# Gathering every unit's cached values by indirect transfer, copying only the keys, and moving the transposes to transfers two units earlier

## The chip, the core and the metric

The kernel runs on one core of a Trainium2 chip. Its metric is the device time of one execution in microseconds. Five engines work side by side, each on its own list of instructions: TensorE (PE in the profile; PEld is its weight load), VectorE (DVE), ScalarE (ACT), GpSimd (POOL) and SyncE (SP), which here only starts transfers. Semaphores order them. Transfers run on 16 DMA engines. They are started by SP and ACT, and, where the addresses come from an index list, by POOL.

## The reference

Two layers with residuals. For each of 8 sequences of 128 tokens with 512 features:

```python
x = x + einsum('bsi,boi->bso', x, weight[adapter_ids])      # one 512x512 matrix per sequence
q = rope(rmsnorm(x Wq^T)); k = rope(rmsnorm(x Wk^T)); v = x Wv^T   # 32 query heads, 8 key heads, D = 128
kc = k_cache[block_table].reshape(b, 512, 8, 128)           # 16 pages of 32 keys per sequence
vc = v_cache[block_table].reshape(b, 512, 8, 128)
scores = q . [kc, k] / sqrt(D), cached keys past cache_seqlens masked; probs = softmax(scores)
x = x + (probs . [vc, v]) Wo^T
```

All is float32, and the kernel keeps that accuracy by splitting each operand into a rounded high part and a low remainder and multiplying three times (high by high, high by low, low by high).

## The kernel before

The attention is cut into 64 units. Unit u is key head u // 8 with its 4 query heads, of sequence u % 8, and has 640 keys: 512 cached and 128 new. A period of the program works on several units at once. In period i TensorE makes the scores of unit i (`scores`), projects the queries and keys of unit i+1 (`project_q`, `project_kv`, then `turn_q` and `turn_k`, which transpose them), multiplies the probabilities of unit i-1 with the values (`times_v`), and projects the output of unit i-2 (`project_o`). The order of every engine's instructions is written out by hand; there is no scheduler.

The probabilities have to be transposed before they meet the values. Up to unit NA-1 (NA is 8) TensorE does it: `turn_p` makes 20 transposes of 128x128 for a unit, and ACT and DVE split what comes out. From unit NA on, ACT and DVE first split the probabilities into two 16-bit planes (`upper_plane` L817, `lower_plane` L1080), SP starts four transposing transfers (`turn_upper` L458, `turn_lower` L470), and ACT (L753) and POOL (`p_lo`, L591) read the turned planes. `LAST` (unit 63) is turned on TensorE again.

The cached keys and values come in one of two ways. Units 0 to 8 (below NL = 9) take them from the pages: SP starts 16 transfers of 16 KB for the keys (`load_kt`), and POOL four indirect gathers of 128 rows of 512 B for the values (`gather_v`, L562), partition p of tile t being key 128t + p. For all later units the kernel first makes a copy in DRAM in the order of the sequences (`copy_page` L338, 16 pages for each sequence, keys and values of the remaining heads in one transfer of 224 KB). ACT then loads a unit's keys (`load_k` L348) and SP its values (`load_v` L443), 256 KB each. The tables COPY_SP and COPY_ACT say how many groups of four pages each engine starts in each period.

GpSimd's work in a period from NA+1 on, in the order of its program, is: a part of a weight chunk if the tables put one at place 0 (`split_w(i, 0)`, which writes wl), the low part of the keys (`keys_lo`, kl), the sum of the two rotary products (`q_sum`, m), the high part of the values (`values_hi`, vh), the scales (`scales`, var and rst), the low part of the values (`values_lo`, vl), three of the five `p_lo` (ptl), a weight chunk at place 1, and the last two `p_lo`. LO_POOL gives the chunks 0 to 9 of key head h the periods 8h-5, 8h-4, 8h-3 (place 1), 8h-2 (places 0 and 1), 8h-1 (place 0), 8h (place 1), 8h+1 (places 0 and 1), and 8h+2 (place 0); LO_DVE moves a few early ones to VectorE, chunks 4 and 5 of head 1 (period 6) among them.

Of the kernel before, what the change touches and what calls it, by code (L numbers as in the profile page):

```python
# [15 lines left out]
P = 128  # L16
NB = 8
# [6 lines left out]
PSZ = 32  # L24
KEYS = 640
# [26 lines left out]
NL = NB + 1  # L52
NA = 8
# [5 lines left out]
COPY_SP = (0, 1, 1, 1, 1, 1, 1, 2, 0, 1, 1, 1, 1, 1)  # L59
COPY_ACT = (2, 2, 3, 2, 2, 3, 3, 2, 1, 0, 0, 0, 0, 0)  # L60
# [39 lines left out]
def build(nc, x, xt, lw, wall, kv, ids_lens, table, pages, qkw, consts, iota, out):  # L100
    with ExitStack() as ctx:
# [9 lines left out]
        def slots(name, n):  # L111
# [57 lines left out]

        inv_s = cst[:, 3:67]  # L170
# [59 lines left out]
        d_k, d_v, d_mask, d_lenc, d_rows = (slots("d_k", 2), slots("d_v", 2), slots("d_mask", 2),  # L230
                                            sem("d_lenc"), sem("d_rows"))
# [5 lines left out]
        c_ilf, c_tabf, c_kidx, c_kidx1, c_pos, c_ang, c_sin, c_cos = (  # L237
            sem("c_ilf"), sem("c_tabf"), sem("c_kidx"), sem("c_kidx1"), sem("c_pos"), sem("c_ang"), sem("c_sin"),
# [29 lines left out]
        copy = nc.dram_tensor("cache_rows", (2 * NK, NB, NPG, PSZ * D), F32, kind="Internal").ap()  # L268
# [52 lines left out]
        def load_kt(e, regs, v, t):  # L321
# [6 lines left out]
            for j in range(4):  # L328
# [3 lines left out]
                    kv[2 * hk + 1, bass.ds(numbers[j], 1), :].rearrange("a (p n) -> (a p) n", p=P)  # L332
                ).then_inc(d_rawk[v % 2], 16)

        def copy_page(e, b, k, number):

            rows = slice(2 if b >= NL - NB else 4, 2 * NK)
            e.dma_start(copy[rows, b, k, :].rearrange("r (s n) -> s r n", s=16),  # L338
                        kv[rows, bass.ds(number, 1), :].rearrange("r a (s n) -> (a s) r n", s=16)
                        ).then_inc(d_copy[b], 16)  # L340

        def load_k(e, v):
            hk, b = divmod(v, NB)
            if v < NL + NB:
# [4 lines left out]
                        copy[2 * hk + 1, b].rearrange("k (d r) -> d k r", r=PSZ)  # L349
# [47 lines left out]
        def _(e):  # L397
# [1303 lines left out]
```

## Time and profile before

| what | value |
|---|---|
| runs | 1002.82, 1002.83, 1006.3 us; median 1002.83 us |
| profiled execution, span from first to last instruction | 1006.6 us |
| TensorE busy | 994.3 us (99%) |
| VectorE busy | 861.5 us (86%) |
| ScalarE busy | 810.3 us (80%) |
| GpSimd busy | 795.8 us (79%) |
| bytes moved by transfers | 180.94 MB |

The profiled execution is one run of its own; no time around its span is given. Busy shares are means over the whole span. The start, the eight or so units in which TensorE transposes, and the long even part after them have different limits, so the trace is read by stretches below. A period of the even part is told in the trace by L1527, the transposing of a unit's new keys, which TensorE does once in each period.

### The profile page before, as it was taken

To read this page: it belongs to the slowest core of one execution; us is meant where nothing else is said; L and a number is where in the kernel's file an instruction comes from. 1 tells how busy PE (TensorE), PEld (TensorE's weight loads), DVE (VectorE), ACT (ScalarE), POOL (GpSimd) and SP (SyncE) were. 2 spreads that over 40 slices of the span, in tenths; PEclk is the share of its full clock that TensorE was granted. 3 is DMA by queue.
4 is the path that set the end of the run, shared out by engine and by line. 5 is a ranking of instruction groups with operands and counts; after the bars stand their busy time and mean duration, and the time that the engine had idled before them with its cause. 6 is when DMAs were issued, how large, how long until landed. Compare 5 with 4: busy or idle time off the path is not lost.

```text
span 1006.6 us, 19441 instructions
## 1 busy us (share of the span) xinstructions
PE 994.3 (99%) x5471; PEld 864.3 (86%) x5471; DVE 861.5 (86%) x1787; ACT 810.3 (80%) x2109; POOL 795.8 (79%) x811
## 2 busy tenths in 40 slices
PE   8999999999999999999999999999999999999998
PEld 6778888888888888888888888888888888888886
DVE  7676657799999899999998999899999999998995
ACT  4455456698889889888988898898888988988884
POOL 4876677497889879897898888898798978888672
PEclk9999999999999999999999999999999999999999
DMA  8999879899988888888988888888988879888873
GB/s 254 277 262 260 283 229 258 213 211 201 221 162 162 161 158 153 166 157 152 171 153 162 156 160 165 148 168 155 170 148 165 157 151 166 162 162 144 153 149 84
DMA packets 513643, 180.94 MB, mean 180 GB/s; under 512 B 429873, under 2 KB 495682, under 8 KB 513538
## 3 DMA queue, kind: packets, MB, share of 16 engines
q1 hardware_dynamic: 381280, 143.20, 68.9%
q10 hardware_dynamic: 131106, 34.15, 15.3%
q0 software_dynamic: 1152, 2.36, 0.8%
q8 instruction: 45, 0.74, 0.3%
q14 instruction: 60, 0.49, 0.2%
HBM read 105.45 MB, written 31.86 MB: 136 GB/s over the span
## 4 chain that ended last, share of the span: by engine, by line
PE 95%; DVE 2%; ACTq 1%; issue 1%; ACT 1%; another core or an unknown queue 0%; POOL 0%; DVEq 0%
PE S L1408 22%; PE O L1341 7%; PE O L1343 7%; PE O L1342 7%; PE Q L1341 6%; PE Q L1343 6%; PE Y L1341 6%; PE Q L1342 6%; PE Y L1343 6%; PE Y L1342 6%; PE T L1347 4%; PE KV L1342 3%; PE KV L1341 3%; PE KV L1343 3%; PE KV L1361 1%; PE Y L1361 1%
## 5 line engine op out<-in xcount | busy, mean ns | idle before, releaser
L1080 DVE SCALAR_TENSOR_TENSOR pr<-pr,rc,raw 128x640 f16<-128x640 f32 x220 | 258.8, 1177 | 15.3 <-ACT raw L817 8.3
L1052 DVE CUSTOM_DVE_ANT_0 pr<-S,mask,rst 128x640 f32<-128x640 f32 x256 | 225.4, 881 | 16.6 <-PE S L1408 13.3
L837 ACT ACTIVATE pr<-pr,nb 128x640 f32<-128x640 f32 x256 | 211.7, 827 | 14.5 <-DVE nb L1052 14.5
L817 ACT ACTIVATE raw<-pr,rc 128x640 f16<-128x640 f32 x220 | 176.2, 826 | 0.6 <-DVE rc L1068 0.4
L617 POOL TENSOR_TENSOR m<-m 128x512 f32<-128x512 f32 x63 | 112.5, 1786 | 73.7 <-DVE m L1119 69.8
L591 POOL TENSOR_SCALAR ptl<-first 128x512 fp32r<-128x512 f16 x140 | 111.8, 799 | 17.6 <-issue 6.0
L570 POOL TENSOR_TENSOR kl<-raw,kh 128x512 fp32r<-128x512 f32 x64 | 97.8, 1528 | 34.5 <-ACT kh L720 33.5
L1408 PE MATMUL S<-kh,qh 128*128 128x320 f32 x512 | 120.8, 317 | 3.7 <-DVE nb L1052 3.6
L591 POOL TENSOR_SCALAR ptl<-turned 128x512 fp32r<-128x512 f16 x135 | 108.3, 802 | 11.2
L1408 PE MATMUL S<-kh,ql 128*128 128x320 f32 x512 | 116.8, 309 | 0.0
L783 ACT ACTIVATE Q<-Q 128x128 f32<-128x128 f32 x256 | 68.2, 266 | 59.9 <-DVE m L1119 59.9
L1408 PE MATMUL S<-kl,qh 128*128 128x320 f32 x512 | 116.2, 308 | 0.0
L1408 PEld LDWEIGHTS S<-kh,qh 128*128 128x128 f32 x512 | 91.7, 189 | 23.8 <-issue 4.7
L1341 PE MATMUL O<-pth,vh 128*128 128x512 f32 x252 | 105.5, 419 | 0.8 <-DVE ptl L983 0.5
L1341 PE MATMUL Y<-wh,oh 128*128 128x512 f32 x252 | 104.7, 415 | 0.4 <-DVE ol L983 0.4
L1341 PE MATMUL Q<-wh,xh 128*128 128x512 f32 x256 | 101.5, 396 | 0.5 <-issue 0.5
L1343 PE MATMUL Q<-wh,xl 128*128 128x512 f32 x256 | 100.9, 394 | 0.0
L1342 PE MATMUL Q<-wl,xh 128*128 128x512 f32 x256 | 100.2, 391 | 0.0
L1342 PE MATMUL Y<-wl,oh 128*128 128x512 f32 x252 | 99.7, 395 | 0.0
L1343 PE MATMUL Y<-wh,ol 128*128 128x512 f32 x252 | 99.6, 395 | 0.0
L1343 PE MATMUL O<-pth,vl 128*128 128x512 f32 x252 | 99.2, 394 | 0.0
L1342 PE MATMUL O<-ptl,vh 128*128 128x512 f32 x252 | 98.6, 391 | 0.0
(179 smaller groups left out, 2674.9 us busy)
## 6 DMA issues: line engine op xcount, KB each, us to landing
wraw<-in_wall SPq DMA_DIRECT2D x74, 256.0 KB, 4.4
cache_rows<-in_kv ACTq DMA_DIRECT2D x80, 224.0 KB
raw<-cache_rows SPq DMA_DIRECT2D x57, 256.0 KB, 4.0
raw<-cache_rows ACTq DMA_DIRECT2D x53, 256.0 KB, 5.0
mask<-mask_rows SPq DMA_DIRECT2D x64, 128.0 KB
cache_rows<-in_kv SPq DMA_DIRECT2D x36, 224.0 KB
first<-in_lw SPq DMA_DIRECT2D x5, 1024.0 KB
cache_rows<-in_kv SPq DMA_DIRECT2D x16, 192.0 KB, 4.2
```

Source lines behind the costliest of these rows:

```text
L570: return e.tensor_tensor(dst, src, hi.bitcast(F32), ALU.subtract)
L591: e.tensor_scalar(ptl[:, i % 3, :].rearrange("p (g n) -> p g n", g=G), plane_tile(u, 1, t), 1.0 / PS, 1.0, ALU.mult, ALU.mult).then_inc(g_ ...
L617: e.tensor_tensor(m1[:, :, :], m1[:, :, :], m2[:, :, :], ALU.add).then_inc(q_added, 1)
L783: made = e.activation(part, part, ACT.Square, accum_out=ssq[:, j % 2, r:r + 1])
L817: e.activation(upper16[:, g, :], pr[:, slot(u, g), :], ACT.Copy, scale=rc[:, u % 2, g:g + 1]).then_inc(a_f1, 1)
L837: e.activation(pr[:, slot(u, g), :], pr[:, slot(u, g), :], ACT.Exp, bias=nb[:, u % 2, g:g + 1], scale=-1.0, accum_out=sm[:, u % 2, g:g + 1 ...
L1052: e.tensor_tensor_reduce(pr[:, slot(u, g), :].rearrange("p (a n) -> p a n", a=2), S[:, :, 0:320], mask[:, u % 2, :].rearrange("p (a n) -> ...
L1080: e.scalar_tensor_tensor(out=lower16(u, g), in0=pr[:, slot(u, g), :], scalar=rc[:, u % 2, g:g + 1], in1=upper16[:, g, :], op0=ALU.mult, op ...
L1341: e.matmul(dst, lh, rh, start=first, stop=False)
L1342: e.matmul(dst, lh, rl, start=False, stop=False)
L1343: return e.matmul(dst, ll, rh, start=False, stop=last)
L1408: made = e.matmul(S[:, a, 0:320], l[:, u % 2, qs], r[:, u % 2, 320 * a:320 * a + 320], start=first, stop=last)
```

## The change

- NA goes from 8 to 6, so units 6 and 7 are transposed by transfers, and NL is NA + 1 = 7, so keys come straight from the pages for units 0 to 6 only.
- `load_v` and its semaphores are gone. POOL gathers the values of all 64 units, with one indirect transfer per unit: 128 rows of 2 KB, four neighbouring keys of a page to a partition. From period 7 on it stands as the last instruction of POOL's period. In the first loop one gather takes the place of four.
- Keys in a tile are thus every fourth key of a page. The page layout of the keys in DRAM, the iota for the mask, ACT's rounding of the keys (`keys_hi`) and POOL's `keys_lo` follow this order: both now read the raw keys in runs of 8 elements.
- The copy in DRAM holds keys alone: 7 rows of 16 KB a page (8 for sequence 7) instead of 14 (12 for part of them), so 112 KB a transfer. COPY_SP and COPY_ACT spread it over 12 periods instead of 14.
- The index list has one column per unit, made on VectorE in eight small steps (`value_rows`) over the first periods, and the table of pages comes in one transfer instead of four.

```diff
-NL = NB + 1
-NA = 8
+NA = 6
+NL = NA + 1
-COPY_SP = (0, 1, 1, 1, 1, 1, 1, 2, 0, 1, 1, 1, 1, 1)
-COPY_ACT = (2, 2, 3, 2, 2, 3, 3, 2, 1, 0, 0, 0, 0, 0)
+COPY_SP = (0, 1, 1, 1, 1, 1, 1, 2, 2, 2, 2, 1)
+COPY_ACT = (2, 3, 3, 3, 3, 3, 0, 0, 0, 0, 0, 0)
...
+        def by_tile(keys):
+
+            return keys.rearrange("d (g t j) -> d t g j", g=NPG, t=NT)
+        def tiles_of(keys):
+            return keys.rearrange("d (t g j) -> d t g j", g=NPG, t=NT)
...
-            rows = slice(2 if b >= NL - NB else 4, 2 * NK)
+            rows = slice((NL - b + NB - 1) // NB, NK)
...
-            def load_v(v):
-                hk, b = divmod(v, NB)
-                if v < NL + NB:
-                    e.wait_ge(d_copy[b], 16 * NPG)
-                e.wait_ge(g_vlo, v - 1 if v <= NA else v)
-                e.dma_start(rawv[raw_at(v)], copy[2 * hk, b].rearrange(
-                    "k (r d) -> (k r) d", d=D).rearrange("(t p) d -> p t d", p=P)
-                            ).then_inc(d_v[v % 2], 16)
...
-                if NL <= i < NU:
-                    load_v(i)
...
-            def gather_v(v, t):
...
+            def gather_v(v):
+                e.wait_ge(c_kidx, v // NB + 1)
+                if v >= 2:
+                    e.wait_ge(g_vlo, v - 1 if v <= NA else v)
                 e.indirect_dma_start(
-                    out=rawv[raw_at(v)][:, t, :], out_offset=None,
...
+                    out=rawv[raw_at(v)].rearrange("p t d -> p (t d)"), out_offset=None, in_=vc,
+                    in_offset=bass.IndirectOffsetOnAxis(ap=kidx[:, v:v + 1], axis=0)
                 ).then_inc(d_rawv[v % 2], 16)
...
-                minus(kl[:, j % 2, 0:512], rawk[raw_at(j)], kh[:, j % 2, 0:512]).then_inc(g_kc, 1)
+                minus(tiles_of(kl[:, j % 2, 0:512]), by_tile(rawk[raw_at(j)]),
+                      tiles_of(kh[:, j % 2, 0:512])).then_inc(g_kc, 1)
...
                 if w < LAST:
                     p_lo(w, 3)
                     p_lo(w, 4)
+                if i < NU:
+                    gather_v(i)
...
-                rounded(kh[:, j % 2, 0:512], rawk[raw_at(j)]).then_inc(a_kc, 1)
+                rounded(tiles_of(kh[:, j % 2, 0:512]), by_tile(rawk[raw_at(j)])).then_inc(a_kc, 1)
...
-            for g in range(4):
-                e.dma_start(tabb[32 * g:32 * g + 32, :],
-                            table[g:g + 1, :].broadcast_to([32, NB * NT])).then_inc(d_tab, 16)
+            e.dma_start(tabb[:, :], table).then_inc(d_tab, 16)
```

GpSimd's list in a period of the even part with a weight chunk on both sides of the end of the period. Before:

```order
L570 TENSOR_TENSOR vl<-raw,vh 128x512
L591 TENSOR_SCALAR ptl<-turned 128x512 x3
L570 TENSOR_TENSOR wl<-wraw,wh 128x512
L591 TENSOR_SCALAR ptl<-turned 128x512 x2
L570 TENSOR_TENSOR wl<-wraw,wh 128x512
L570 TENSOR_TENSOR kl<-raw,kh 128x512
L617 TENSOR_TENSOR m<-m 128x512
L602 TENSOR_SCALAR vh<-raw 128x512
```

The same place now:

```order
L556 TENSOR_TENSOR vl<-raw,vh 128x512
L577 TENSOR_SCALAR ptl<-first 128x512 x3
L556 TENSOR_TENSOR wl<-wraw,wh 128x512
L577 TENSOR_SCALAR ptl<-first 128x512 x2
L550 DMA raw<-in_vc,kidx 128x512
L556 TENSOR_TENSOR wl<-wraw,wh 128x512
L556 TENSOR_TENSOR kl<-raw,kh 128x512
L601 TENSOR_TENSOR m<-m 128x512
L585 TENSOR_SCALAR vh<-raw 128x512
```

The gather of the next values is added behind the last two ptl, and all that follows on GpSimd stands behind it. Nothing is removed from this list.

TensorE's list ahead of the transposing of the keys of unit 8, in period 7 (m is the rotated query, k the key, pr the probabilities). Before:

```order
L1347 MATMUL T<-ident,m 128x128 x4
L1341 MATMUL O<-pth,vh 128x512
L1342 MATMUL O<-ptl,vh 128x512
L1343 MATMUL O<-pth,vl 128x512
L1341 MATMUL Y<-wh,oh 128x512
L1342 MATMUL Y<-wl,oh 128x512
L1343 MATMUL Y<-wh,ol 128x512
L1408 MATMUL S<-kh,qh 128x320 x2
L1408 MATMUL S<-kl,qh 128x320 x2
L1408 MATMUL S<-kh,ql 128x320 x2
L1347 MATMUL T<-ident,pr 128x128 x8
L1527 MATMUL KV<-ident,k 128x128
```

The same place now:

```order
L1316 MATMUL Y<-wh,oh 128x512
L1317 MATMUL Y<-wl,oh 128x512
L1318 MATMUL Y<-wh,ol 128x512
L1383 MATMUL S<-kh,qh 128x320 x2
L1383 MATMUL S<-kl,qh 128x320 x2
L1383 MATMUL S<-kh,ql 128x320 x2
L1502 MATMUL KV<-ident,k 128x128
```

The transposes of pr are gone from this period (12 more of them stood further ahead in the list before), and the products with the values are ordered as in the even part.

## Rows read from the trace of the kernel before

**Rows 1.** The page: the span, and busy time of each engine.
```profile
span 1006.6 us, 19441 instructions
PE 994.3 (99%) x5471; PEld 864.3 (86%) x5471; DVE 861.5 (86%) x1787; ACT 810.3 (80%) x2109; POOL 795.8 (79%) x811
```
**Rows 2.** The page: the chain that ended last, by engine.
```profile
PE 95%; DVE 2%; ACTq 1%; issue 1%; ACT 1%; another core or an unknown queue 0%; POOL 0%; DVEq 0%
```
**Rows 3.** Stretches: length, busy PE, PEld, DVE, ACT, POOL; clock, DMA share, GB/s.
```profile
173.86:190.58 16.72, 16.72 (x103) 14.93 (x102) 11.47 (x28) 11.53 (x32) 9.32 (x11) 1.00 0.94 255
190.58:206.82 16.24, 15.06 (x82) 12.79 (x81) 14.08 (x30) 12.17 (x33) 9.76 (x10) 1.00 0.81 151
395.58:410.10 14.52, 14.52 (x82) 12.80 (x80) 13.24 (x28) 13.16 (x36) 13.57 (x14) 1.00 0.88 153
```
**Rows 4.** Groups by form: count, busy us, mean ns, idle before.
```profile
L1347 PE MATMUL T<-ident,pr 128*128 128x128 f32 x172 | 23.0, 272 | 0.2 <-DVE pr L1072 0.2
L983 DVE TENSOR_TENSOR wl<-wraw,wh 128x512 fp32r<-128x512 f32 x11 | 8.3, 794 | 0.0
```
**Rows 5.** GpSimd in order of time, one full interval: start, us, instruction, idle before.
```profile
434.79 0.20 POOL L632 TENSOR_SCALAR var<-ssq 128x5 f32<-128x5 f32 x1 [0.19 <-ACT KV L788]
...
436.22 1.29 POOL L570 TENSOR_TENSOR vl<-raw,vh 128x512 fp32r<-128x512 f32 x1
437.60 2.47 POOL L591 TENSOR_SCALAR ptl<-first 128x512 fp32r<-128x512 f16 x3
440.15 1.30 POOL L570 TENSOR_TENSOR wl<-wraw,wh 128x512 fp32r<-128x512 f32 x1
441.53 1.78 POOL L591 TENSOR_SCALAR ptl<-first 128x512 fp32r<-128x512 f16 x2
443.39 1.31 POOL L570 TENSOR_TENSOR wl<-wraw,wh 128x512 fp32r<-128x512 f32 x1
444.65 1.89 POOL L570 TENSOR_TENSOR kl<-raw,kh 128x512 fp32r<-128x512 f32 x1
446.65 1.87 POOL L617 TENSOR_TENSOR m<-m 128x512 f32<-128x512 f32 x1
...
449.31 0.20 POOL L632 TENSOR_SCALAR var<-ssq 128x5 f32<-128x5 f32 x1 [0.20 <-ACT KV L788]
```
**Rows 6.** TensorE in order of time, where it takes GpSimd's results.
```profile
440.63 0.40 PE L1341 MATMUL O<-pth,vh 128*128 128x512 f32 x1
...
449.53 0.60 PE L1347 MATMUL T<-ident,m 128*128 128x128 f32 x4
```
**Rows 7.** GpSimd's waits, 395.58 to 511.74: us in total, times, longest.
```profile
POOL m L617 <- DVE m L1119: 8.6, 4, 2.3
```
**Rows 8.** GpSimd in order of time, two gathers of the first loop.
```profile
114.07 1.28 POOL L570 TENSOR_TENSOR kl<-raw,kh 128x512 fp32r<-128x512 f32 x1 [2.46 <-ACT kh L720]
115.50 1.05 POOL L562 DMA_INDIRECT raw<-in_kv,kidx  x1 [0.16 <-issue]
116.86 0.94 POOL L562 DMA_INDIRECT raw<-in_kv,kidx  x1 [0.30 <-issue]
117.85 0.81 POOL L580 TENSOR_SCALAR pr<-pr,rc 128x640 f32<-128x640 f32 x1
```
**Rows 9.** Single lines: duration in ns, min/median/max, first and last start.
```profile
L570 POOL TENSOR_TENSOR kl<-raw,kh x64: 1255/1303/1910, 24.4 to 965.6; 128x512 fp32r<-128x512 f32 x64
...
L617 POOL TENSOR_TENSOR m<-m x63: 1268/1868/1875, 33.4 to 969.3; 128x512 f32<-128x512 f32 x63
...
L1080 DVE SCALAR_TENSOR_TENSOR pr<-pr,rc,raw x220: 868/1294/1725, 190.7 to 982.8; 128x640 f16<-128x640 f32 x110
```
**Rows 10.** Landing: of POOL's transfers into raw, and of the 256 KB loads.
```profile
DMA to landing us min/median/max: 3.2/4.7/6.9
...
raw<-cache_rows SPq DMA_DIRECT2D x57, 256.0 KB, 4.0
raw<-cache_rows ACTq DMA_DIRECT2D x53, 256.0 KB, 5.0
```

More of the change, by code:

```diff
@@ L24 @@
 PSZ = 32
+VK = 4
+ROWS = PSZ // VK
 KEYS = 640
@@ L97, in copies_of, with build @@
             for k in range(first, first + (COPY_ACT if act else COPY_SP)[period])]
-def build(nc, x, xt, lw, wall, kv, ids_lens, table, pages, qkw, consts, iota, out):
+def build(nc, x, xt, lw, wall, kc, vc, ids_lens, table, pages, qkw, consts, iota, out):
     with ExitStack() as ctx:
@@ L265, in build @@
         a_norm, v_norm = sem("a_norm"), sem("v_norm")
-        copy = nc.dram_tensor("cache_rows", (2 * NK, NB, NPG, PSZ * D), F32, kind="Internal").ap()
+        copy = nc.dram_tensor("cache_rows", (NK, NB, NPG, PSZ * D), F32, kind="Internal").ap()
         mask_rows = nc.dram_tensor("mask_rows", (NB, NT * P), BF16, kind="Internal").ap()
@@ L348, in load_k @@
             e.dma_start(rawk[raw_at(v)].rearrange("d (k r) -> d k r", r=PSZ),
-                        copy[2 * hk + 1, b].rearrange("k (d r) -> d k r", r=PSZ)
+                        copy[hk, b].rearrange("k (d r) -> d k r", r=PSZ)
                         ).then_inc(d_k[v % 2], 16)
@@ L519, in _ @@
                     load_k(e, i + 2)
-                for n, (b, t) in enumerate(copies_of(i)):
-                    if n == 2 and NL <= i + 2 < NA:
-                        load_v(i + 2)
+                for b, t in copies_of(i):
                     copy_pages(b, t)
-                if len(copies_of(i)) <= 2 and NL <= i + 2 < NA:
-                    load_v(i + 2)
             for i in range(NA, NU + 2):
@@ L595, in values_hi @@
             def values_hi(u):
-                if u < NL:
-                    e.wait_ge(d_rawv[u % 2], 64 * (u // 2 + 1))
-                else:
-                    e.wait_ge(d_v[u % 2], 16 * ((u - NL) // 2 + 1))
+                e.wait_ge(d_rawv[u % 2], 16 * (u // 2 + 1))
                 if u >= 2:
@@ L657, in _ @@
             e.wait_ge(c_mhalf, 1)
-            for t in range(NT):
-                gather_v(0, t)
-            for t in range(2):
-                gather_v(1, t)
+            gather_v(0)
+            gather_v(1)
             for i in range(-1, NA + 1):
@@ L1213, in _ @@
                 turn = w >= 0
-                if i == 2:
-                    key_rows_1()
+                for hk in range(2 * i - 1, 2 * i + 1):
+                    if 1 <= hk < NK:
+                        value_rows(hk)
                 if o >= 0:
```

79 lines of the change are left out of this document (30 added, 49 removed).

## Prediction

> **What bounds the kernel now.** I read the page first. TensorE is busy 99% of a span of 1006.6 us [rows 1], and 95% of the chain that ended last is TensorE's own work [rows 2]. So time is gained only by taking work from TensorE, and lost where another engine makes it wait. Then I read stretches [rows 3]. A late period in which TensorE still turns the probabilities takes 16.72 us, a period of the even part 14.52, both with TensorE busy from end to end. The period between the two, where the program changes over, takes 16.24 with 15.06 busy. The even part runs from period 10 to 62 without a wait on TensorE that I can see, so its 14.52 us is a wall of work, and the question there is who is near that wall. In the same rows GpSimd is busy 13.57 of 14.52 us. Its timeline shows the rest [rows 5]: from one var (434.79) to the next (449.31) it stands still only 0.20 us, waiting for ACT. That is an interval with two weight chunks (wl). By LO_POOL such intervals come in pairs: two in a row, then intervals with none or one chunk. In 395.58 to 511.74, eight periods, the sum m waited for VectorE only 4 times, 8.6 us in all [rows 7]; the other four intervals are full.
>
> **What the change takes away.** Units 6 and 7 are no longer turned on TensorE: 2 x 20 of the transposes of [rows 4]. Priced by the periods: 16.72 - 14.52 = 2.20 us a unit, so 4.4 us off TensorE's list. At 99% busy all of it counts. The values' half of the copy and the 256 KB loads by SP go as well, 57 loads of 256 KB are 14.9 MB [rows 10]; no engine's wait in the even part hangs on them, so they count 0. They land 4.0 us after issue, far ahead of their use. SP loses one issue and one wait a period, also 0.
>
> **The change-over.** It moves from period 8 to period 6. It now meets two chunks that VectorE splits in period 6, 2 x 0.794 us [rows 4]. In the period that stands there before, VectorE is busy 11.47 of 16.72 [rows 3], so they may hide wholly (0). But in the following one TensorE already loses 16.24 - 15.06 = 1.2 us behind VectorE, and then all of 1.6 could be added. I take the middle, +0.8. The start changes little: three fewer issues on ACT, no wait that they end on TensorE's side that I can name, 0 (bounds -1.5 and +0.5).
>
> **What the change adds: a gather on GpSimd in every period of the even part.** Two gathers with nothing between them ran from the end of kl (114.07 + 1.28 = 115.35) to the next instruction at 117.85 [rows 8], so 1.25 us each, for 128 rows each. The new ones have 128 rows too, four times as long; the engine makes the same number of descriptors, so I take 1.25. Four times as much is the far bound if the cost went by bytes, which I hold unlikely.
>
> Where does 1.25 us fit? In intervals with no chunk or one, m waits about 2 us for VectorE anyway and the gather disappears. In a full interval there is 14.52 - 0.20 = 14.32 us of work, and 14.32 + 1.25 = 15.57, that is 1.05 over. Behind the gather stand wl, kl, m, vh, var, rst and vl; TensorE waits for m (turning the query) and for ptl (products with the values). Slack: m ends at 446.65 + 1.87 = 448.52 and is used at 449.53 [rows 5, 6], 1.0 us; the third ptl ends at 437.60 + 2.47 = 440.07 and is used at 440.63, 0.56 us. The second is smaller and counts. A pair of full intervals ends 2 x 1.05 = 2.1 us late; TensorE forgives 0.5 and waits 1.6. The light interval after the pair takes up what is left. Pairs from period 7 on: periods (8h+1, 8h+2) for h = 1 to 7 and (8h-2, 8h-1) for h = 2 to 7, 13 in all. 13 x 1.6 = 20.8 us.
>
> This price has two uncertain parts. First, ports. kl takes 1303 ns at the median and 1910 at most, m 1268 at least and 1868 at the median, and VectorE's L1080, the only frequent one with two large inputs in SBUF, from 868 to 1725 [rows 9]; in the full interval kl takes 1.89 and m 1.87 [rows 5]. So they get in each other's way by about 0.6 us at a time, and moving GpSimd's work by 1.25 us moves who meets whom. If both kl and m came free, 1.2 us would return in each full interval and the loss would be 0. If a wl or ptl more were hit, another 0.6 per interval, 2.8 us a pair and 36 us in all.
>
> Second, the new order of reading. kl and ACT's kh read the raw keys in runs of 8. No row shows such a read on either engine. I take 0, since the step inside a run is one element; below 0 is excluded, as the element count is the same; above, kl at its slowest (1.91 for 1.30, +0.6) is the nearest row and gives the same 36 us bound.
>
> The Trainium skill (SBUF — State Buffer, the part on port contention) says that a VectorE instruction with two SBUF inputs and a GpSimd instruction that reads SBUF take an exclusive lock from each other, and infers that making descriptors, which only writes, is not shut out. The rows on kl, m and L1080 agree with the first half. By the second the gather would be a window in which L1080 runs free, and the total would be that of the first rival below.
>
> **Sum.** The profiled execution has 1006.6 us: 1006.6 - 4.4 + 0.8 + 20.8 = 1023.8. It stands 3.8 us above the median of the runs, 1002.83, and near the slowest, 1006.3; the terms do not depend on that, so against the median 1002.83 + 17.2 = 1020.0 us.
>
> **Rival 1, GpSimd takes it in: not slower.** In a full interval L1080 runs beside the gather instead of beside kl, and m, moved past the L1080 that now stretches it, is back at 1.27. Then each full interval gains 2 x 0.6 and pays 1.25, and TensorE stays at 14.52. Time 1002.83 - 4.4 + 0.8 = 999.2. It decides as soon as the pair ends less than the 0.5 us slack late. For it: TensorE has no wait at all there today. Against it: behind the gather come wl and kl, both with two inputs, and they move onto the L1080s that kl and m leave.
>
> **Rival 2, the values land too late: much slower.** The gather stands at the end of the period, and vh, which needs it, 4.9 to 6.2 us of GpSimd's work later. GpSimd's own chain from vh to the next gather takes about 9.5 us with a chunk in it (434.79 to 441.53 + 1.78 = 443.31 is 8.5, and vh ahead of it and the step to the gather 1.0) [rows 5], so a landing later than 14.5 - 9.5 = 5.0 us lengthens the interval. The gathers of 64 KB land in 3.2 to 6.9, median 4.7 us [rows 10], the direct 256 KB loads in 4.0 and 5.0. With 4.7 it fits. With 6.5 us it is 1.5 over in six of eight intervals: some 20 pairs x (3.0 - 0.5) = 50 us, 1002.83 - 3.6 + 50 = 1049.
>
> The Trainium skill's page DMA: Bandwidth & Descriptors (Anatomy of one DMA — SWDGE path) fits about 2.0 us plus bytes over 436 GB/s, an estimate of 2.6 us for 256 KB. The traced landing of a quarter of these bytes is 4.7, so the fit, which would rule this rival out, does not hold beside this traffic.
>
> **Rival 3, the cost of the gather goes by bytes.** Between 1.25 and 5 us, say 2.5: then even light intervals fill, GpSimd's mean of about 13.2 us a period (14.32 less a mean of 1.1 of idle) becomes 15.7, and 53 periods lose 1.2 each: 1002.83 - 3.6 + 64 = 1063.
>
> **Chances.** Forecast 0.60, Rival 1 0.25, Rival 2 0.08, Rival 3 0.03, and 0.04 for something at the start or in the copies. The forecast's own range is 1006 to 1035. The range given, 999 to 1036, takes in most of Rival 1 and leaves out Rivals 2 and 3 and a little on the low side. A change within 0.5% (5 us) can't be told from none here. Faster by more than that needs below 997.8: 0.09, the best part of Rival 1. Within it: 0.16 of Rival 1, 0.07 of the forecast, 0.02 else, 0.25. Slower: 0.66.
>
> **What would show it.** In the changed profile: pr transposes on T 132 instead of 172; periods from 7 on of 14.52 us where GpSimd has no or one chunk, and two long ones for each pair, with waits of TensorE for GpSimd's ptl or m (pth/O and T), none of which stands in the trace before; a gather of about 1.05 us on GpSimd each period; GpSimd without idle time in the pairs. I am wrong if all periods stay at 14.52 (Rival 1), if vh waits for the transfer (Rival 2), or if the gather takes 2 us or more (Rival 3).

## The result: slower by 8.4%, five times the loss that was forecast

| | before | changed |
|---|---|---|
| runs, median | 1003.4 us (1002.82 to 1006.3, 4 runs) | 1088.51 us (1086.2 to 1091.44, 4 runs) |
| ratio | | 1.084, 95% interval 1.0815 to 1.0865 |
| profiled span | 1006.6 us | 1089.6 us |

The direction was right. The forecast, 1020.0 us, and its range to 1036, were not: the kernel lost 85 us where 17 were forecast.

The page of the changed kernel, the lines that answer to [rows 1, 2], and its costliest group:

```profile
span 1089.6 us, 19308 instructions
PE 1013.7 (93%) x5431; PEld 871.8 (80%) x5431; DVE 971.2 (89%) x1795; ACT 816.9 (75%) x2117; POOL 816.0 (75%) x841
...
PE 37%; DVE 24%; issue 21%; ACT 11%; DMA 3%; ACTq 1%; POOL 1%; SPq 0%; DVEq 0%; POOLq 0%
...
L1053 DVE SCALAR_TENSOR_TENSOR pr<-pr,rc,raw 128x640 f16<-128x640 f32 x228 | 359.3, 1576 | 9.5 <-ACT raw L794 7.2
```

TensorE's share of the last chain fell from 95% to 37%, and VectorE's rose from 2% to 24%. GpSimd, which got the new work, has 1%: a row of VectorE that waits for GpSimd counts as VectorE's time. VectorE's busy time grew by 110 us although its list grew by only eight instructions. Nearly all of it is in L1053 (`lower_plane`, L1080 before): 1576 ns each for 228, where it was 1177 (258.8 us for 220). TensorE shows 1013.7 us busy with 40 instructions fewer, a sign of a slower clock.

Stretches of the changed kernel, each from one transposing of the new keys to the next (columns as in [rows 3]). The intervals of GpSimd in them hold 0, 2, 2, 0, 1, 1, 2 and 2 weight chunks:

```profile
432.75:447.25 14.50, 14.50 (x82) 12.77 (x80) 13.80 (x28) 12.33 (x33) 11.65 (x13) 1.00 0.83 162
447.25:465.65 18.40, 16.31 (x83) 14.30 (x80) 16.01 (x28) 13.84 (x37) 15.31 (x17) 0.91 0.76 140
465.65:481.09 15.44, 14.79 (x83) 12.86 (x80) 14.07 (x27) 12.59 (x33) 12.64 (x13) 1.00 0.67 137
481.09:495.61 14.52, 14.52 (x83) 12.79 (x80) 13.78 (x28) 12.33 (x33) 11.67 (x13) 1.00 0.79 157
495.61:511.18 15.57, 14.78 (x82) 12.87 (x80) 15.15 (x28) 12.96 (x36) 12.64 (x14) 1.00 0.77 143
511.18:526.87 15.69, 14.79 (x83) 12.86 (x81) 15.41 (x28) 12.76 (x34) 12.76 (x14) 1.00 0.77 161
526.87:543.81 16.94, 14.72 (x82) 12.85 (x80) 16.66 (x28) 13.16 (x35) 14.01 (x15) 1.00 0.65 133
543.81:560.76 16.95, 14.73 (x82) 12.86 (x80) 16.66 (x28) 12.90 (x34) 14.02 (x15) 1.00 0.73 130
```

Three things stand here. The periods with one chunk, which I took for free, lose 1.1 us. Those with two lose 2.4 (only 0.9 in the third line, where VectorE asks later after the delay). And one of them, 18.40 us, has a granted clock of 0.91: TensorE, back from a wait, ran part of the period at 1.2 instead of 2.4 GHz, so the same list took 16.31 busy us, and that period lost 3.9.

Where it is lost, GpSimd in order of time in the period from 447.25, to be held against [rows 5]:

```profile
448.35 1.29 POOL L556 TENSOR_TENSOR wl<-wraw,wh 128x512 fp32r<-128x512 f32 x1
449.72 1.78 POOL L577 TENSOR_SCALAR ptl<-turned 128x512 fp32r<-128x512 f16 x2
451.78 1.09 POOL L550 DMA_INDIRECT raw<-in_vc,kidx  x1 [0.28 <-issue]
452.90 1.30 POOL L556 TENSOR_TENSOR wl<-wraw,wh 128x512 fp32r<-128x512 f32 x1
454.16 1.28 POOL L556 TENSOR_TENSOR kl<-raw,kh 128x512 fp32r<-128x512 f32 x1
457.41 1.84 POOL L601 TENSOR_TENSOR m<-m 128x512 f32<-128x512 f32 x1 [1.97 <-DVE m L1092]
```

VectorE over the same time:

```profile
452.43 3.70 DVE L1053 SCALAR_TENSOR_TENSOR pr<-pr,rc,raw 128x640 f16<-128x640 f32 x1 [0.28 <-ACT raw L794]
456.05 0.68 DVE L1088 TENSOR_TENSOR m<-Q,tab 128x512 f32<-128x512 f32 x1
456.65 0.67 DVE L1092 TENSOR_TENSOR m<-Q,tab 128x512 f32<-128x512 f32 x1
457.25 0.87 DVE L1053 SCALAR_TENSOR_TENSOR pr<-pr,rc,raw 128x640 f16<-128x640 f32 x1
458.05 0.87 DVE L1025 CUSTOM_DVE_ANT_0 pr<-S,mask,rst 128x640 f32<-128x640 f32 x1
```

And TensorE:

```profile
458.98 0.86 PE L1383 MATMUL S<-kh,qh 128*128 128x320 f32 x2 [2.09 <-DVE nb L1025]
```

L1053 starts 0.65 us into the gather and lasts until 456.13. Undisturbed it takes 0.87, so it did its work from about 455.26, when kl was ending, and was held for 2.8 us before. It slipped in neither between gather and wl nor between wl and kl. Then the rotary products are late, and with them GpSimd's m (it waits 1.97 us, in its busiest interval) and `largest` (L1025), whose nb TensorE waits for. Most of TensorE's waiting is of this kind, and the longest of GpSimd's (its m waited for VectorE before too, 69.8 us in 32 times):

```profile
PE S L1383 <- DVE nb L1025: 61.7, 42, 2.3
...
POOL m L601 <- DVE m L1092: 117.0, 58, 4.1
...
POOL vh L585 <- DMA raw<-in_vc,kidx: 10.1, 7, 3.9
```

The single lines that answer to [rows 9, 10], min/median/max in ns, and the gathers' landing in us:

```profile
L556 POOL TENSOR_TENSOR kl<-raw,kh x64: 1257/1285/1884, 24.9 to 1043.5; 128x512 fp32r<-128x512 f32 x64
L601 POOL TENSOR_TENSOR m<-m x63: 1267/1838/1874, 34.3 to 1046.8; 128x512 f32<-128x512 f32 x63
L1053 DVE SCALAR_TENSOR_TENSOR pr<-pr,rc,raw x228: 867/1290/4052, 159.3 to 1060.0; 128x640 f16<-128x640 f32 x114
L550 POOL DMA_INDIRECT raw<-in_vc,kidx x64: 958/1099/1162, 12.5 to 1068.6; - x64
DMA to landing us min/median/max: 3.5/4.5/7.8
```

The longest L1080 before was 1.725 us; the longest L1053 is 4.052, and the median has not moved.

### The profile page after: what moved, and what is told of

Same layout as the page of the kernel before. It is cut to its first block, busy times and chain, and to the rows that moved or that the text cites. A ratio compares the mean times of both kernels' runs of the same rounds, so it can differ in the third digit from the quotient of the medians.

```text
span 1089.6 us, 19308 instructions
## 1 busy us (share of the span) xinstructions
PE 1013.7 (93%) x5431; PEld 871.8 (80%) x5431; DVE 971.2 (89%) x1795; ACT 816.9 (75%) x2117; POOL 816.0 (75%) x841
## 4 chain that ended last, share of the span: by engine, by line
PE 37%; DVE 24%; issue 21%; ACT 11%; DMA 3%; ACTq 1%; POOL 1%; SPq 0%; DVEq 0%; POOLq 0%
PE S L1383 9%; DVE pr L1053 9%; DVE pr L1025 5%; DVE k L1123 3%; PE Y L1316 3%; PE Y L1317 3%; ACT raw L794 3%; PE Y L1318 3%; DVE m L1092 2%; PE T L1322 2%; PE O L1316 2%; PE O L1317 2%; PE O L1318 2%; PE Q L1316 2%; ACT pr L814 2%
## 5 line engine op out<-in xcount | busy, mean ns | idle before, releaser
L1053 DVE SCALAR_TENSOR_TENSOR pr<-pr,rc,raw 128x640 f16<-128x640 f32 x228 | 359.3, 1576 | 9.5 <-ACT raw L794 7.2
L1025 DVE CUSTOM_DVE_ANT_0 pr<-S,mask,rst 128x640 f32<-128x640 f32 x256 | 224.8, 878 | 22.4 <-PE S L1383 19.2
L814 ACT ACTIVATE pr<-pr,nb 128x640 f32<-128x640 f32 x256 | 210.8, 824 | 12.8 <-DVE nb L1025 12.6
L794 ACT ACTIVATE raw<-pr,rc 128x640 f16<-128x640 f32 x228 | 182.2, 823 | 6.8 <-DVE rc L1041 6.4
L1383 PE MATMUL S<-kh,qh 128*128 128x320 f32 x512 | 125.1, 325 | 61.8 <-DVE nb L1025 61.7
L577 POOL TENSOR_SCALAR ptl<-first 128x512 fp32r<-128x512 f16 x145 | 115.6, 797 | 14.4 <-issue 1.6
L577 POOL TENSOR_SCALAR ptl<-turned 128x512 fp32r<-128x512 f16 x140 | 111.1, 794 | 12.8 <-issue 1.4
L1316 PE MATMUL Y<-wh,oh 128*128 128x512 f32 x252 | 108.4, 430 | 0.3 <-DVE ol L958 0.3
L1317 PE MATMUL Y<-wl,oh 128*128 128x512 f32 x252 | 102.1, 405 | 0.0
L556 POOL TENSOR_TENSOR kl<-raw,kh 128x512 fp32r<-128x512 f32 x64 | 82.8, 1294 | 20.4 <-ACT kh L697 19.5
```

Source lines behind the costliest of these rows:

```text
L556: return e.tensor_tensor(dst, src, hi.bitcast(F32), ALU.subtract)
L577: e.tensor_scalar(ptl[:, i % 3, :].rearrange("p (g n) -> p g n", g=G), plane_tile(u, 1, t), 1.0 / PS, 1.0, ALU.mult, ALU.mult).then_inc(g_ ...
L794: e.activation(upper16[:, g, :], pr[:, slot(u, g), :], ACT.Copy, scale=rc[:, u % 2, g:g + 1]).then_inc(a_f1, 1)
L814: e.activation(pr[:, slot(u, g), :], pr[:, slot(u, g), :], ACT.Exp, bias=nb[:, u % 2, g:g + 1], scale=-1.0, accum_out=sm[:, u % 2, g:g + 1 ...
L1025: e.tensor_tensor_reduce(pr[:, slot(u, g), :].rearrange("p (a n) -> p a n", a=2), S[:, :, 0:320], mask[:, u % 2, :].rearrange("p (a n) -> ...
L1053: e.scalar_tensor_tensor(out=lower16(u, g), in0=pr[:, slot(u, g), :], scalar=rc[:, u % 2, g:g + 1], in1=upper16[:, g, :], op0=ALU.mult, op ...
```

## The experiments

Lines are given by name, since their numbers differ from kernel to kernel. In the texts on record L1053 is `lower_plane` of the changed kernel and L1080 that of the kernel before, sp_load is the version of the next paragraph, and joined the one with memset and wait. Ratios are to the kernel before on the same chip, with 95% intervals.

### Is it the gather at all?

**No gather.** SP loads the values from unit 7 on in one plain transfer of the same size, in place of the gathers.

```diff
+                e.dma_start(rawv[raw_at(v)].rearrange("p t d -> p (t d)"),
+                            vc[64 * ROWS * hk:64 * ROWS * hk + P, :]).then_inc(d_v[v % 2], 16)
...
+                if NA < i < NU:
+                    load_v(i)
...
-                if i < NU:
-                    gather_v(i)
```

> The changed kernel, but from unit 7 on SP loads the values with one plain transfer of 256 KB from fixed rows of the values (the page table is left out for them), and GpSimd gathers nothing there. Theory A (the gather stands on GpSimd's list and, through the SBUF access that GpSimd and VectorE share, makes VectorE's L1053 wait until GpSimd's list stands still): L1053 falls from a mean of 1576 ns to about 1180, all even periods are 14.5 us again, and the time is that of before less the transposes, 997 to 1001 us. Theory B (GpSimd simply has too much work): the same, 997 to 1001. Theory C (the strided reading of the keys by ACT and GpSimd, or the smaller copies, are to blame): still above 1060 us.

Measured: 1010.66 us, ratio 1.004 (1.0027 to 1.0052). `lower_plane` is back at 1165 ns, and every period from 13 on is 14.52. So about 78 of the 85 us come with the gather; the strided keys, the key-only copy and the two units turned by transfers don't make them, and theory C is out. Theories A and B both wanted 997 to 1001 us and missed by 10. Part of what is left stands at the change-over, which comes below.

**The gather alone**, added to the kernel before: 128 rows of 64 bytes into a tile that nobody reads, at the end of each GpSimd period.

```diff
+                if i < NU:
+                    e.indirect_dma_start(
+                        out=extra[:, :], out_offset=None,
+                        in_=kv.rearrange("c a (r d) -> (c a r) d", d=16),
+                        in_offset=bass.IndirectOffsetOnAxis(ap=kidx[:, 0:1], axis=0)
```

> The kernel before with one more indirect gather per period on GpSimd, from period 9 on, at the place where the changed kernel has it: 128 rows of 64 B into a tile that nobody reads. Theory A: the gather alone makes the loss, whatever its bytes: periods with a weight chunk at place 1 take 15.4 to 17 us as in the changed kernel, L1080 has a mean near 1550 ns, and the time is 1003 + about 85 = 1080 to 1095 us. Theory C: stays at 1003 to 1008. Theory B, by the forecast's sum, about 1024.

Measured: 1081.61 us, ratio 1.0747 (1.0725 to 1.0768), with `lower_plane` at 1592 ns and the same periods of 14.52, 15.6, 15.7 and 17.0. That is theory A's range. The bytes are 1/32 of those of the real gather, and nobody waits for their landing except the next of these gathers, so neither bytes nor landing make the loss.

### Is it GpSimd's time, or what the gather does to VectorE?

**As much time, but no gather**: five chained memsets of about 1.1 us together in its place, in the version with SP's loads.

```diff
+                    for n in range(5):
+                        if i > NA + 1 or n:
+                            e.wait_ge(c_idle, 5 * (i - NA - 1) + n)
+                        e.memset(cst[:, :], 0.0).then_inc(c_idle, 1)
```

> The kernel of sp_load with five small memsets in a row (each waits for the one before, together about 1.1 us) on GpSimd where the gather was. They write SBUF but read nothing. Theory B (time on GpSimd's list is what costs): as slow as the changed kernel, about 1085 us. Theory A: what the gather does beyond its time is missing, VectorE gets in between GpSimd's instructions, and the time is 1000 to 1025 us (at most the 20 us of the forecast's sum for a list that is 1.05 us too long).

Measured: 1021.2 us, ratio 1.0146 (1.0126 to 1.0167), 10.5 us more than without them. One-chunk periods stay at 14.52, pairs of full ones take 15.08 and 14.90, together 0.94 us over the wall, where 1.6 was forecast. So theory B is out: as much time on GpSimd's list, without the gather, costs an eighth of the loss. And even this isn't the wait of the forecast. Between 250 and 980 us TensorE waits 5.3 us in 19 times for VectorE's nb, and never for m or ptl.

**The gather, but VectorE's other input from PSUM**: `lower_plane` of units 7 to 62 reads its second operand from the accumulator memory (PSUM) and no longer two large ones from SBUF. What it reads there is old contents of a bank, so this kernel leaves the low parts of the probabilities out.

```diff
-                    in1=upper16[:, g, :], op0=ALU.mult, op1=ALU.subtract)
+                    in1=T[:, 0, 0:320].unsqueeze(1).broadcast_to([P, 2, 320]),
+                    op0=ALU.mult, op1=ALU.subtract)
```

> The changed kernel with L1053 of units 7 to 62 reading its second input from PSUM (old contents of a bank) instead of from SBUF, so that it has one input in SBUF; the low parts of the probabilities are thereby wrong. Theory A: L1053 takes 0.87 to 0.9 us every time, also beside the gather, and nothing else delays VectorE: 995 to 1010 us. Theory B: GpSimd's list is as long as before, so the periods with chunks stay above 15.4 us and the time stays above 1060.

Measured: 1017.63 us, ratio 1.0111 (1.0072 to 1.015). Two full intervals of this kernel, with gather and two chunks:

```profile
428.29:442.82 14.53, 14.53 (x82) 12.80 (x81) 12.44 (x28) 13.18 (x36) 12.79 (x16) 1.00 0.91 178
442.82:457.34 14.52, 14.52 (x82) 12.79 (x80) 12.40 (x27) 13.16 (x36) 12.60 (x15) 1.00 0.78 153
```

`lower_plane` takes 876 ns throughout. The time is 8 us above theory A's range and far below theory B's; what is over is mostly right behind the change-over, where two periods take 18.87 and 17.19 us. GpSimd is busy 12.6 to 12.8 of 14.52 us with everything on its list. The forecast had 14.32 us of work there before the gather's 1.25. That first term was wrong: the rows of that interval sum to 13.66 us, and the same rows here to 11.56 (the gather adds 1.09). The 2.1 us between them were waiting for VectorE inside the rows of kl, m and ptl (kl takes 1.27 here and 1.89 in [rows 5], m 1.29 and 1.87, the five ptl 3.34 and 4.25), while wl takes 1.30 in both.

### Why is VectorE held so long?

One simpler reading is that the gather only moves VectorE's request to a worse place. The two traces rule it out. In the kernel before, `lower_plane` was asked for 25 times while wl ran with kl right behind it, 0.4 to 0.8 us before wl's end. Each time it got in between the two, and took 1.1 to 1.5 us. In the changed kernel seven requests came at such a place behind a gather, about 0.6 us before wl's end. Each was held through kl as well, 2.51 to 2.57 us. One of each, asked for 0.92 us into the wl of 443.39 [rows 5], and 0.71 us into a wl at 469.89:

```profile
444.31 1.07 DVE L1080 SCALAR_TENSOR_TENSOR pr<-pr,rc,raw 128x640 f16<-128x640 f32 x1 [0.35 <-ACT raw L817]
470.60 2.53 DVE L1053 SCALAR_TENSOR_TENSOR pr<-pr,rc,raw 128x640 f16<-128x640 f32 x1 [0.66 <-ACT raw L794]
```

The two theories from here on. D: behind a gather GpSimd's processors go on out of step, so that there is no common gap for VectorE until GpSimd really waits for something. E: only requests that VectorE makes during the gather are held.

**Gather, memset, wait for the memset.**

```diff
                     gather_v(i)
+                    e.memset(cst[:, 0:8], 0.0).then_inc(c_join, 1)
+                    e.wait_ge(c_join, i - NA)
```

> The changed kernel with one memset of 8 elements behind each gather of the even part, for whose completion GpSimd waits before it goes on. Theory D (after a gather GpSimd's cores are out of step, since a few of them make the descriptors and the others go ahead, so that between the following instructions there is no moment at which all have let go of the SBUF access, until GpSimd has to wait for something): the wait brings the cores together, L1053 falls from 1576 ns to about 1200, and the time to that of sp_memset and sp_load together, 1018 to 1028 us. Theory E (only a VectorE request that comes while the gather itself runs is held): the request still comes in it, so the periods stay long, above 1070 us.

Measured: 1032.27 us, ratio 1.0275 (1.0238 to 1.0312), 4 us above D's range and far below E's. `lower_plane` has a mean of 1198 ns. Two small edits give back 56 of 85 us. GpSimd in a one-chunk period:

```profile
480.20 1.11 POOL L551 DMA_INDIRECT raw<-in_vc,kidx  x1 [0.28 <-issue]
481.31 0.12 POOL L694 MEMSET cst<- 128x8 f32 x1
481.52 1.27 POOL L557 TENSOR_TENSOR kl<-raw,kh 128x512 fp32r<-128x512 f32 x1
483.08 1.87 POOL L602 TENSOR_TENSOR m<-m 128x512 f32<-128x512 f32 x1 [0.28 <-DVE m L1095]
```

VectorE there:

```profile
480.51 0.88 DVE L1056 SCALAR_TENSOR_TENSOR pr<-pr,rc,raw 128x640 f16<-128x640 f32 x1
```

It starts 0.3 us into the gather, as most of the held ones did (26 of the changed kernel's start 0.31 or 0.32 us into it), and runs at once. So the gather itself doesn't hold it, and E as stated is out. The seven requests above say the same, since they came when the gather was over. And in the changed kernel two requests came 1.02 us into a gather: the one with kl behind the gather took 2.10 us, the one behind whose gather GpSimd had to wait 3.94 us took 0.89.

**The memset without the wait.** GpSimd waits only for the memset of the period before, long done.

```diff
+                    e.wait_ge(c_join, i - NA - 1)
+                    e.memset(cst[:, 0:8], 0.0).then_inc(c_join, 1)
```

> The changed kernel with a memset of 8 elements behind each gather of the even part, but without GpSimd waiting for that memset to finish (it waits only for the memset of the period before, long done); output complete. It tells apart two readings of why the version with memset and wait lost only 29 us where the changed kernel loses 85. Theory D (GpSimd has to come to a stop behind the gather, so that all of it starts the next instruction together; without a stop VectorE's lower_plane finds no gap until GpSimd waits for m): 1075 to 1090, the longest lower_plane about 4 us, as in the changed kernel. Rival W (it is enough that something other than a two-input instruction stands right behind the gather, as the ptl does in the version with the gather before the last ptl, 1033.5): 1026 to 1038, the longest lower_plane at most 2 us.

Measured: 1092.8 us, ratio 1.0887 (1.0843 to 1.0931), 3 us above D's range; the longest `lower_plane` is 4.10 us. W is out. GpSimd:

```profile
450.58 1.09 POOL L551 DMA_INDIRECT raw<-in_vc,kidx  x1 [0.28 <-issue]
451.67 0.12 POOL L696 MEMSET cst<- 128x8 f32 x1
451.74 1.31 POOL L557 TENSOR_TENSOR wl<-wraw,wh 128x512 fp32r<-128x512 f32 x1
453.00 1.27 POOL L557 TENSOR_TENSOR kl<-raw,kh 128x512 fp32r<-128x512 f32 x1
456.24 1.84 POOL L602 TENSOR_TENSOR m<-m 128x512 f32<-128x512 f32 x1 [1.97 <-DVE m L1096]
```

VectorE:

```profile
451.21 3.76 DVE L1057 SCALAR_TENSOR_TENSOR pr<-pr,rc,raw 128x640 f16<-128x640 f32 x1 [0.26 <-ACT raw L798]
```

Same instructions, same order, and the hold is back. wl starts 0.05 us before the memset's row ends, while in the version that waits the next instruction starts 0.09 after it. It is the waiting for completion that lets VectorE in; an instruction in between does nothing. With the waiting comes a pause of about 0.1 us, and these two versions don't tell the one from the other.

**The gather before the last ptl** instead of behind it.

```diff
                     p_lo(w, 3)
+                if i < NU:
+                    gather_v(i)
+                if w < LAST:
                     p_lo(w, 4)
-                if i < NU:
-                    gather_v(i)
```

> The changed kernel with the gather one place earlier, between the fourth and the fifth ptl, so that no L1053 begins while the gather runs. Theory E: L1053 about 1200 ns and 1018 to 1030 us. Theory D: the following ptl, wl and kl still run without a common gap until GpSimd waits for m, L1053 stays near 1550 ns and the time above 1070 us.

Measured: 1033.53 us, ratio 1.0274 (1.0246 to 1.0301). D wanted over 1070 and missed; E's range was missed by 3.5 us, and its mean of 1200 ns by 62. The longest `lower_plane` is 1.98 us. In 24 periods it is asked for in the last 0.3 us of the gather and takes 0.88. In 14 it is asked for while the ptl runs that now follows the gather, and is done in 1.05 to 1.18, before wl: 0.67 us after the ptl's end, as in the kernel before, where 17 requests during a ptl ended 0.67 us after it too. So a ptl doesn't leave the port open; VectorE waits for its end, but then gets in. Whether a ptl brings GpSimd back into step, these runs don't tell. What they do tell: the hold needs wl or kl straight behind the gather (a memset between doesn't count) and no real wait between.

### What is the rest?

**The copies spread evenly**, in the version with SP's loads: SP starts one group a period instead of two in periods 7 to 10, ACT takes the others earlier.

```diff
-COPY_SP = (0, 1, 1, 1, 1, 1, 1, 2, 2, 2, 2, 1)
-COPY_ACT = (2, 3, 3, 3, 3, 3, 0, 0, 0, 0, 0, 0)
+COPY_SP = (0, 1, 1, 1, 1, 1, 1, 1, 1, 1, 1, 1)
+COPY_ACT = (3, 3, 3, 3, 3, 3, 3, 0, 0, 0, 0, 0)
```

> The kernel of sp_load with the copying of the pages spread otherwise: SP starts one group of four in each of periods 1 to 11 (before: two groups in periods 7 to 10), ACT three in periods 0 to 6. If SP's own list, full in periods 7 to 11, is what makes ptl late there (6.6 us of waiting in periods 9 to 12), those periods fall to 14.5 to 16.2 us and the time to 1002 to 1006 us. If it is the DMA engines or the two units turned earlier, it stays at 1009 to 1012.

Measured: 1006.14 us, ratio 0.999 (0.997 to 1.001), 4.5 us less, at the upper end of the range for SP's list. The first periods after the change-over, with the copies as in the changed kernel:

```profile
189.65:205.46 15.81, 14.75 (x83) 12.86 (x80) 13.81 (x27) 13.47 (x37) 11.71 (x12) 1.00 0.94 212
205.46:222.59 17.13, 15.01 (x83) 12.64 (x80) 14.14 (x28) 13.11 (x34) 13.06 (x13) 1.00 1.02 188
```

and spread evenly:

```profile
189.59:204.11 14.52, 14.52 (x82) 12.79 (x80) 13.19 (x28) 13.16 (x36) 13.52 (x14) 1.00 0.97 207
204.11:218.63 14.52, 14.52 (x82) 12.80 (x80) 13.21 (x28) 13.16 (x36) 13.54 (x14) 1.00 0.91 181
```

SP in one of the long periods, the copies ahead of the transposing transfers (seven of the eight are in this window; the second line is the load of values, which only the versions with SP's loads have):

```profile
189.67 5.85 SPq L347 DMA_DIRECT2D cache_rows<-in_kc  x7
195.57 0.58 SPq L450 DMA_DIRECT2D raw<-in_vc  x1
196.25 1.62 SPq L464 DMA_TRANSPOSE first<-raw  x1
```

Eight copies and four transposing transfers nearly fill SP's period, in the changed kernel too (from 187.99 to 202.45). The turned planes come late, and TensorE waits for ptl, 4.1 us in five waits between 180 and 260.

**Both**: the version with memset and wait, copies spread evenly.

> Both edits on the changed kernel, all values from the pages. Theory D and SP's list together: 1011 to 1021 us, 5 to 8 us below joined. Theory E: above 1065.

Measured: 1025.08 us, ratio 1.0193 (1.0173 to 1.0212), 4 us above the range of D. The copies give 7 us here, 5.1 of them from unit 8 to 12. What remains are pairs of about 15.1 us. One full interval of GpSimd:

```profile
430.83 1.44 POOL L557 TENSOR_TENSOR wl<-wraw,wh 128x512 fp32r<-128x512 f32 x1
432.24 1.28 POOL L557 TENSOR_TENSOR kl<-raw,kh 128x512 fp32r<-128x512 f32 x1
433.47 1.87 POOL L602 TENSOR_TENSOR m<-m 128x512 f32<-128x512 f32 x1
```

VectorE there:

```profile
432.24 1.96 DVE L1056 SCALAR_TENSOR_TENSOR pr<-pr,rc,raw 128x640 f16<-128x640 f32 x1
434.13 0.87 DVE L1028 CUSTOM_DVE_ANT_0 pr<-S,mask,rst 128x640 f32<-128x640 f32 x1
```

kl, moved back by the gather, starts at the same moment as the second `lower_plane` of the period, which takes 1.96 instead of 0.87. nb is late, and TensorE waits 0.38 us. In the kernel before, it took 0.87 in the same place, and kl's successor m was the one that waited. So in full intervals too TensorE waits for VectorE, and not for m or ptl.

**No full intervals.** Added to that: VectorE makes four weight chunks a head, so that GpSimd never has two. Three versions, first with the chunks 3, 5, 7 and 9.

```diff
-LO_DVE = {(0, 6): (1, 0), (0, 7): (1, 1), (0, 9): (2, 0), (1, 4): (-2, 1), (1, 5): (-2, 1)}
+LO_DVE = {(0, 6): (1, 0), (0, 7): (1, 1), (0, 9): (2, 0), (1, 4): (-2, 1), (1, 5): (-2, 1),
+          3: (-2, 0), 5: (-1, 0), 7: (1, 0), 9: (2, 0)}
-LO_POOL = {(0, 8): (1, 1), 0: (-5, 1), 1: (-4, 1), 2: (-3, 1), 3: (-2, 0), 4: (-2, 1),
-           5: (-1, 0), 6: (0, 1), 7: (1, 0), 8: (1, 1), 9: (2, 0)}
+LO_POOL = {(0, 8): (1, 1), 0: (-5, 1), 1: (-4, 1), 2: (-3, 1), 4: (-2, 1),
+           6: (0, 1), 8: (1, 1)}
```

> The version with memset, wait and the copies spread evenly (1025.1), and in it the weight chunks 3, 5, 7 and 9 of key heads 1 to 7 made by VectorE (0.79 us each) instead of GpSimd, so that no interval of GpSimd has two chunks; output complete. It tells apart where the remaining 20 us come from. Theory F (from the full intervals alone: with two chunks and the gather, kl comes 1.7 us later, meets the fourth-row lower_plane and TensorE waits 0.3 to 0.4 us for nb, twice a pair, with part of a halved clock behind it): no period of the even part over 14.6 except where VectorE now has the chunk, 1002 to 1010. Rival V (VectorE is as near its end as GpSimd; the chunk of 0.79 us on it makes nb as late as before): four periods a head of 15.1 to 15.4, 1020 to 1032.

Measured: 1030.21 us, ratio 1.0252 (1.0225 to 1.0279). Both theories missed: the time lies in V's range, but the waits are not V's. The pairs are gone, nearly all periods 14.52 (the others 15.15 at most), but in six periods VectorE's chunk 5 comes too late for the product of the new keys with it: 13.3 us of waits, 2.2 at a time, each ending 0.1 us after that chunk, and periods of 16.9 to 18.5 there.

Then chunk 5 one place earlier on VectorE:

```diff
-          3: (-2, 0), 5: (-1, 0), 7: (1, 0), 9: (2, 0)}
+          3: (-2, 0), 5: (-2, 1), 7: (1, 0), 9: (2, 0)}
```

> The version with memset and wait, even copies, and chunks 3, 5, 7 and 9 made by VectorE (1030.2), with chunk 5 one place earlier on VectorE; output complete. In that version all periods that were long in pairs had become 14.52, and six periods had a new wait of 2.2 us at TensorE, for the product of the new keys and values with chunk 5. Theory F (the full intervals were all that was left of the loss beside the completion hold and SP's list): the six waits go, nearly all periods from 8 on are 14.52, 1000 to 1007. Rival V (VectorE has no room for four chunks a head, and now two of them stand near each other): waits of TensorE for nb or for the chunk in each head, 1012 to 1028.

Measured: 1030.23 us, ratio 1.022 (1.0191 to 1.025). Missed again, by both. Now VectorE stands 1.9 us before chunk 5, whose high part ScalarE makes later in that period, and TensorE waits 1.3 to 2.1 us for nb, once a head.

Last, chunk 5 back on GpSimd, at its old place, and chunk 4 on VectorE:

```diff
-          3: (-2, 0), 5: (-2, 1), 7: (1, 0), 9: (2, 0)}
-LO_POOL = {(0, 8): (1, 1), 0: (-5, 1), 1: (-4, 1), 2: (-3, 1), 4: (-2, 1),
-           6: (0, 1), 8: (1, 1)}
+          3: (-2, 0), 4: (-2, 1), 7: (1, 0), 9: (2, 0)}
+LO_POOL = {(0, 8): (1, 1), 0: (-5, 1), 1: (-4, 1), 2: (-3, 1),
+           5: (-1, 0), 6: (0, 1), 8: (1, 1)}
```

> The version with memset and wait, even copies, and four chunks a head made by VectorE, now 3, 4, 7 and 9, with chunk 5 back on GpSimd; output complete. The last version (chunk 5 on VectorE, 1030.2) still had one long period a head: VectorE stood 1.9 us waiting for ScalarE's high part of chunk 5 and TensorE then 1.3 to 2.1 us for nb; all pairs of long periods were gone. Chunk 4's high part is made one place of ScalarE earlier. Theory F (the pairs were all that was left of the loss): no such wait, nearly all periods from 8 on 14.52, 1000 to 1007, the same as the kernel before within 0.5%. Rival V (VectorE has no room for a chunk there): one wait for nb of 0.5 to 1 us a head stays, 1010 to 1018.

Measured: 1011.41 us, ratio 1.0048 (1.0031 to 1.0065). From period 8 to 62 eight periods take more than 14.56 us, the longest 15.11. The pairs, and the waits that the two earlier tables made, were what remained in the middle of the program. Theory F's 1000 to 1007 us were missed by 4; the time lies in V's range, but V's wait for nb, once a head, isn't there (one of 0.9 us between 130 and 975). By the table below the profiled execution is 2.9 us longer than that of before: 3.3 at the end, where TensorE waits 2.3 us for the last unit's vl, whose gather now stands at the end of GpSimd's last full period, 2.4 ahead of unit 8, 1.1 in the middle, and 3.9 less from unit 8 to 12.

## Why the prediction was wrong

The spans of the profiled executions, cut at the transposing of the new keys of units 8, 12 and 63, in us:

| | to 8 | 8 to 12 | 12 to 63 | end | span |
|---|---|---|---|---|---|
| before | 173.9 | 62.0 | 740.5 | 30.2 | 1006.6 |
| changed | 175.1 | 63.4 | 814.9 | 36.2 | 1089.6 |
| memset and wait | 174.2 | 64.4 | 754.8 | 33.3 | 1026.8 |
| and even copies | 173.4 | 59.3 | 755.3 | 33.9 | 1021.8 |
| and no full intervals | 176.3 | 58.1 | 741.6 | 33.5 | 1009.5 |
| no gather, even copies | 175.1 | 58.1 | 740.5 | 30.4 | 1004.0 |

The direction came out, but not by the mechanism of the forecast: in the changed kernel TensorE waits 0.9 us in all for GpSimd's ptl, never for GpSimd's m, and 61.7 us for VectorE's nb. So the right sign was luck.

- **Transposes, -4.4: right.** Without the other terms the stretch from 8 to 12 fell from 62.0 to 58.1, -3.9, and TensorE's busy time from 994.3 to 989.6.
- **Change-over, +0.8: too small.** I looked at VectorE's two chunks, and they cost nothing that shows (the period of the change-over takes 15.95 us with even copies, 16.24 before). SP's list did, with two copy groups beside four transposing transfers: +4.5 us by the two versions with SP's loads, and 64.4 - 59.3 = 5.1 by the two with memset and wait. I had written that SP loses one issue a period and so costs 0, and never summed its list for the periods in which the copies and the transposing transfers now meet.
- **The step that failed: the price of the ports.** I bounded a collision by the rows, 0.6 us [rows 9], and the whole by 36 us. Those rows were taken where VectorE finds a gap after each GpSimd instruction. With wl or kl straight behind a gather it finds none until GpSimd waits, so the hold is a chain of instructions long: 1.9 or 3.2 us over the 0.87 where it is asked for 0.3 us into the gather, with one or two chunks in the interval (2.8 and 4.05 in all). Without a chunk it is asked for after the gather, when kl has just begun, and the 1.96 there is a wait for kl alone, as versions without the hold show it too. Taken away alone, the hold returned 56 of 85 us, and it hits the one-chunk periods that I had put at 0. From unit 12 to 63 the changed kernel takes 814.9 - 740.5 = 74.4 us more: 55.4 are waits of TensorE, and 19.0 are longer busy time for the same list. Part of the latter is the clock, as in the period with 0.91 granted (1.00 over this stretch before, 0.99 here).
- **Full intervals, 20.8: too large, and wrong in mechanism.** With hold and copies out of the way the pairs cost 755.3 - 741.6 = 13.7 us by the table. But GpSimd's list wasn't full (12.7 of 14.52 us once `lower_plane` had one input from PSUM), and the delay reached TensorE through nb, at most 0.5 us at a time (8.5 us in 23 waits), and some 0.2 us of longer busy time, not through m or ptl with their slack of 0.5 to 1.0.
- **The end, not in the sum: +3,** and +6.0 in the changed kernel itself. SP had loaded the last values early; the gather stands behind five ptl, and TensorE waits for it (2.9 us for the last vl in the changed kernel).
- **The gather itself: 1.10 us** at the median for the 1.25 assumed, so Rival 3 is out. **Rival 2** is a detail: vh waited for its transfer 7 times, 10.1 us in all on GpSimd, and with a median landing of 4.5 us, close to the 4.7 assumed. **The strided keys** cost nothing (kl 1285 ns for 1303 at the median, ScalarE's kh 622 for 627 in the mean).
- **Rival 1** had the sign of the port effect wrong. It said that VectorE runs free beside a gather. That half is true: in the version that waits, 0.88 us beside the gather. The Trainium skill (SBUF — State Buffer, Who interferes with whom) infers that making descriptors leaves such an instruction free, and that trace agrees. What follows the gather undoes it.

For the hold the runs give the conditions, and not what happens inside GpSimd. The Trainium skill (GPSIMD Engine Reference, Instruction dispatch) says that each of the engine's processors starts the next instruction once it has finished its own share, and that completion holds back only what waits on the semaphore. With the lock on the port that would do it: processors that had nothing to do in the gather would go on to wl, and from then on one or another would always hold the port. That the wait cures it and the memset alone doesn't speaks for this; the version with the gather before the last ptl isn't explained by it without more. No run here looked at single processors, so this reading stays argued.

No version beat the kernel before. The one without a gather and with even copies, which reads fixed rows and not those of the page table, is the same within the noise (0.999). Of those with the real gather the best stays 0.5% slower.

## What to carry to other kernels

A duration in a trace contains the waiting inside it. Before a list is called full, price its rows by their shortest durations, and before a collision is priced by the slowest row, ask whether the change keeps the gaps that ended it. When an indirect transfer is put on GpSimd between instructions that share a port with VectorE, let GpSimd wait for a completion behind it, or put it where GpSimd waits anyway. And where a change lets two kinds of transfers meet on one queue, sum that queue's list for those periods.

## What was not expected of the hardware

- After an indirect transfer on GpSimd, a VectorE instruction with two SBUF inputs was held through up to two following GpSimd instructions, 4.05 us for 0.87 of work. Between the same two instructions without a gather ahead it got in (1.1 to 1.5 us). With a wait for the completion of an 8-element memset in between it took 0.88.
- A gather of 128 rows takes 1.1 us on GpSimd whether a row is 64 bytes or 2 KB, and a VectorE instruction with two SBUF inputs took 0.88 us beside it where GpSimd waited behind it.
- A wait of about 2 us of TensorE was followed by a lower granted clock in some periods (0.91 over 18.40 us, 1.8 us more busy time for the same list) and not in others of the same kind (1.00 over 16.94 us).
